# Attention inside a two-layer kernel on one core: where the maximum is subtracted, how the rows are summed, and when they are divided

## What is computed

```python
q = _split_heads(query @ Wq.T + bq)          # 16 heads, D_K = 8
k = _split_heads(key @ Wk.T + bk)
v = _split_heads(value @ Wv.T + bv)
scores = jnp.einsum('bhqd,bhkd->bhqk', q, k) / np.sqrt(D_K)
scores = jnp.where(mask[:, None, :, :] == 0, jnp.float32(-1000000000.0), scores)
p_attn = jax.nn.softmax(scores, axis=-1)
attn = jnp.einsum('bhqk,bhkd->bhqd', p_attn, v)
x = attn.transpose(0, 2, 1, 3).reshape(B, S, D_MODEL)
return x @ Wo.T + bo
```

## Time and profile before

| | |
|---|---|
| median of three runs | 1567.44 us |
| the profiled execution: its own time (span) | 1567.5 us |
| TensorE matmul busy | 1337.5 us |
| VectorE busy | 1011.9 us |
| ScalarE busy | 872.6 us |
| GpSimd busy | 716.2 us |
| mean granted TensorE clock | 0.921 |

### The profile page before, as it was taken

The page is one execution under the profiler, slowest core; times in us unless marked ns, Lnnn a source line. Parts: engine busy times, 40 slices in busy tenths (PEclk is TensorE's granted clock), DMA queues, the critical chain, the costliest instruction groups (busy, mean ns, idle before and its releaser), DMA issues.

```text
span 1567.5 us, 25069 instructions
## 1 busy us (share of the span) xinstructions
PE 1337.5 (85%) x6350; PEld 979.1 (62%) x6350; DVE 1011.9 (65%) x2377; ACT 872.6 (56%) x2421; POOL 716.2 (46%) x971
## 2 busy tenths in 40 slices
PE   7778988889978898879888899888998898896884
PEld 5556766667656766557666676666666576574552
DVE  6866675856668476766758566585666857574442
ACT  5535764556744575447655466455664477553652
POOL 3533554435534355444634355344553446442342
PEclk9979997999989899999989899799997999996765
DMA  3310000000000000000000000000000000000000
GB/s 99 108 41 4 5 9 15 4 6 7 5 14 4 7 8 6 16 6 8 4 20 2 9 4 10 14 4 8 8 6 14 5 9 5 6 3 7 4 4 4
DMA packets 34084, 20.48 MB, mean 13 GB/s; under 512 B 3624, under 2 KB 31888, under 8 KB 33936
## 3 DMA queue, kind: packets, MB, share of 16 engines
q1 hardware_dynamic: 33936, 18.81, 4.2%
HBM read 16.70 MB, written 2.10 MB: 12 GB/s over the span
## 4 chain that ended last, share of the span: by engine, by line
PE 45%; DVE 20%; issue 15%; POOL 10%; ACT 8%; DVEq 1%; POOLq 0%; SPq 0%; DMA 0%; ACTq 0%
PE M L1034 5%; PE U L1051 5%; PE U L877 4%; DVE h_lo L743 4%; PE U L881 4%; PE U L878 4%; PE Y L877 3%; ACT big L648 3%; PE Y L881 3%; PE M L1021 3%; DVE h L739 3%; PE Y L878 2%; PE M L1041 2%; PE M L1065 2%; POOL big L549 2%
## 5 line engine op out<-in xcount | busy, mean ns | idle before, releaser
L743 DVE TENSOR_TENSOR h_lo<-h,h_hi 128x512 fp32r<-128x512 f32 x384 | 316.9, 828 | 72.6 <-POOL h_hi L508 60.0
L508 POOL TENSOR_SCALAR h_hi<-h 128x512 fp32r<-128x512 f32 x256 | 180.5, 707 | 257.7 <-ACT h L609 230.0
L648 ACT ACTIVATE big<-big,nmax 128x128 f32<-128x128 f32 x512 | 199.8, 395 | 88.8 <-DVE nmax L841 88.3
L609 ACT ACTIVATE h<-U,biasT 128x512 f32<-128x512 f32 x256 | 175.9, 687 | 102.5 <-PE U L881 88.9
L549 POOL TENSOR_TENSOR big<-big,rinv 128x512 f32<-128x512 f32 x128 | 150.3, 1174 | 151.7 <-DVE rinv L844 151.7
L1051 PE MATMUL U<-big,Vr 128*128 128x512 f32 x256 | 150.9, 674 | 24.0 <-ACT big L653 24.0
L1034 PEld LDWEIGHTS M<-kT,qT 8*128 8x128 f32 x944 | 116.1, 189 | 84.3 <-issue 69.6
L1034 PE MATMUL M<-kT,qT 8*128 8x128 f32 x944 | 138.7, 286 | 2.2 <-ACT sg L666 2.1
L877 PE MATMUL U<-xn_hi,w_hi 128*128 128x512 f32 x256 | 119.3, 466 | 21.9 <-DVE h L739 12.9
L844 DVE RECIPROCAL rinv<-rsum 128x4 f32<-128x4 f32 x128 | 22.7, 177 | 174.4 <-ACT big L648 174.4
L619 ACT ACTIVATE h_hi<-h 128x512 fp32r<-128x512 f32 x128 | 80.9, 632 | 84.6 <-DVE h L739 81.7
(11 more groups left out here) (210 smaller groups left out, 3023.9 us busy)
## 6 DMA issues: line engine op xcount, KB each, us to landing
big<-in_L_xattn_W SPq DMA_DIRECT2D x16, 256.0 KB, 3.0
big<-in_L_ffn_w SPq DMA_DIRECT2D x12, 256.0 KB, 2.8
xin<-in_x SPq DMA_DIRECT2D x8, 256.0 KB, 2.7
nat<-in_ctx SPq DMA_DIRECT2D x8, 256.0 KB, 3.2
ctx<-in_ctx SPq DMA_DIRECT2D x32, 64.0 KB, 1.8
mask_sb<-in_mask_BxSxS_if SPq DMA_DIRECT2D x32, 64.0 KB, 1.9
out_dram<-xatt SPq DMA_DIRECT2D x32, 64.0 KB, 1.6
big<-in_L_ffn_w_down SPq DMA_DIRECT2D x1, 176.0 KB
```

The costliest lines, as they stand in the source:

```text
L508: nc.gpsimd.tensor_scalar(h_hi[i % 4][:, :], h32[i % 3][:, :], 1.0, 0.0, ALU.mult, ALU.add).then_inc(hi_done, 1)
L609: nc.scalar.activation(h32[i % 3][:, :], U[i % 2][:, :], ACT.Relu, bias=biasT[:, i:i + 1]).then_inc(relu_done, 1)
L648: done = nc.scalar.activation(p, p, ACT.Exp, bias=nmax[:, u % 2, r:r + 1], accum_out=rsum[:, u % 2, r:r + 1])
L743: nc.vector.tensor_tensor(h_lo[i % 4][:, :], h32[i % 3][:, :], h_hi[i % 4][:, :].bitcast(fp32), ALU.subtract).then_inc(lo_done, 1)
```

## The change

The `exp` step now runs on GpSimd and ScalarE: GpSimd adds the negative maximum to the 128x512 block in place, and ScalarE takes one exponential over the whole block without a sum. The step `rsum` is gone. The transposes wait for the exponential. The `pv` step multiplies the blocks as they are, not yet normalised, in eight matmuls instead of one: for each head h the product with its 32 columns of `Vr` into rows 32h to 32h+31 of `OA` (now 128 columns wide), and then for each head the product with a strip of `ones_r` into the same rows of `OS`, the next 128 columns of the same bank. The strip has ones in the 8 columns that belong to unit r, so that `OS` collects each head's row sum in the same places as `OA` its values. The `ot` step moves to VectorE: reciprocal of `OS`, times `OA`. The exponential stands at half step 2 after the scores in both tables, where two of four stood at 1 before.

```diff
-      "s": (4, 7, 11, 14), "exp": (1, 1, 2, 2), "rsum": 2, "pt": 5, "pv": 7, "ot": 21, "wo": 25,
+      "s": (4, 7, 11, 14), "exp": 2, "pt": 5, "pv": 7, "ot": 21, "wo": 25,
...
-      "s": (5, 8, 11, 15), "exp": (1, 1, 2, 3), "rsum": 3, "pt": 5, "pv": 7, "ot": 22, "wo": 24,
+      "s": (5, 8, 11, 15), "exp": 2, "pt": 5, "pv": 7, "ot": 22, "wo": 24,
...
-        nmax, rsum, rinv = (sb(n, [P, 2, HB]) for n in ("nmax", "rsum", "rinv"))
+        nmax = sb("nmax", [P, 2, HB])
+        ones_r = sb("ones_r", [P, 32 + 3 * DK])
...
-        OA = U[2]
+        OA, OS = U[2][:, 0:P], U[2][:, P:2 * P]
...
-                    elif what == "rsum":
-
-                        pool.wait_ge(rsum_done, g1 * H + (i + 1))
+                    elif what == "exp":
+
+                        pool.wait_ge(nmax_done, g1 * H + (i + 1))
                         p = pr[i % 2].rearrange("p (h k) -> p h k", h=HB)
-                        nc.gpsimd.tensor_tensor(p, p, rinv[:, i % 2, :].unsqueeze(2).broadcast_to([P, HB, S]), ALU.mult).then_inc(norm_done, 1)
+                        nc.gpsimd.tensor_tensor(p, p, nmax[:, i % 2, :].unsqueeze(2).broadcast_to([P, HB, S]), ALU.add).then_inc(shifted, 1)
...
-                        u, r = i // HB, i % HB
-                        if r == 0:
-                            act.wait_ge(nmax_done, g1 * H + (u + 1))
-                        p = pr[u % 2][:, r * S:(r + 1) * S]
-                        done = nc.scalar.activation(p, p, ACT.Exp, bias=nmax[:, u % 2, r:r + 1], accum_out=rsum[:, u % 2, r:r + 1])
-                        if r == HB - 1:
-                            done.then_inc(exp_done, 1)
+                        act.wait_ge(shifted, g1 * H + (i + 1))
+                        nc.scalar.activation(pr[i % 2], pr[i % 2], ACT.Exp).then_inc(exp_done, 1)
...
-                    elif what == "ot":
-
-                        act.wait_ge(oa_full, g1 * TG + (i + 1))
-                        for q in range(HB):
-                            rows = slice(32 * q, 32 * q + 32)
-                            done = nc.scalar.activation(OT[rows, :], OA[rows, q * P:(q + 1) * P], ACT.Copy)
-                        done.then_inc(oa_emptied, 1)
...
+            setup(nc.vector.memset(ones_r[:, :], 0.0))
+            nc.vector.memset(ones_r[:, 3 * DK:4 * DK], 1.0)
...
-                    elif what == "rsum":
-                        dve.wait_ge(exp_done, g1 * H + (i + 1))
-                        nc.vector.reciprocal(rinv[:, i % 2, :], rsum[:, i % 2, :]).then_inc(rsum_done, 1)
+                    elif what == "ot":
+                        dve.wait_ge(oa_full, g1 * TG + (i + 1))
+                        link1(nc.vector.reciprocal(OT[:, :], OS))
+                        nc.vector.tensor_tensor(OT[:, :], OA, OT[:, :], ALU.mult).then_inc(oa_emptied, 1)
...
-                            pe.wait_ge(norm_done, g1 * H + (i + 1))
+                            pe.wait_ge(exp_done, g1 * H + (i + 1))
...
-                        ins = nc.tensor.matmul(OA[:, :], Vr[:, r, :], pT[i % 2], start=(r == 0), stop=(r == HB - 1))
+                        for dst, w in ((OA, Vr[:, r, :]), (OS, None)):
+                            for h in range(HB):
+                                rows = slice(32 * h, 32 * h + 32)
+                                ins = nc.tensor.matmul(dst[rows, :], w[:, rows] if w is not None else ones_r[:, (3 - r) * DK:(3 - r) * DK + 32], pT[i % 2][:, h * P:(h + 1) * P],
+                                                       start=(r == 0 and w is not None), stop=(r == HB - 1), skip_group_check=True)
```

More of the change, by code:

```diff
@@ L37 @@
 Z_SETUP, M_SETUP = 1, 4
-CHAIN0, CHAINP, CHAIN1 = 3, 3, 52
+CHAIN0, CHAINP, CHAIN1 = 3, 3, 56
 CHAIN_GATES = 2
@@ L145, in attention_order @@
             put(t + first, "s", u)
-            for h, later in enumerate(where["exp"]):
-                put(t + first + later, "exp", u * HB + h)
-            for what in ("rsum", "pt", "pv"):
+            for what in ("exp", "pt", "pv"):
                 put(t + first + where[what], what, u)
@@ L309, in flamingo_kernel @@
         cap_made, oa_full, oa_emptied = sem("cap_made"), sem("oa_full"), sem("oa_emptied")
-        nmax_done, exp_done, rsum_done, norm_done = sem("nmax_done"), sem("exp_done"), sem("rsum_done"), sem("norm_done")
+        nmax_done, shifted, exp_done = sem("nmax_done"), sem("shifted"), sem("exp_done")
         pool_gates, pool_passed, dve_passed = sem("pool_gates"), sem("pool_passed"), sem("dve_passed")
```

## The result

The changed kernel takes 1629.49 us (median of four runs, 1626.71 to 1633.8) against 1567.18 us for the kernel before on the same chip: a ratio of 1.0386, with an interval of 1.0348 to 1.0423. It is **62 us slower**. The forecast was 1527 us, faster. The time lies inside the range (1485 to 1650), but only because the range reached up to a rival (strips that don't overlap, 1644 us) which, as will be seen, isn't what happened.

The account below looks back on a forecast made before the run. The prediction held the first attention stretch nearly bound by TensorE, the others by one unit's time from scores to product. From 1567.5 us: 41 less relief, 8 more division, 7 less product, giving 1527 us; range 1485 to 1650.

Parts of the forecast that it names:

- The way through the unit: Attention unit, from end of maximum to transposes: 3.15 us before, 1.9 us after, so 1.2 us less.
- The relief of 41 us: Shorter exponentials and end-of-group waits: 5 us less in each of seven walks, 6 in the last; bounds nothing to 68 us.
- The product on PE: Product with values and ones in strips on TensorE: 0.77 us a unit instead of 0.86, 7 us less altogether.
- 9.4 units of 16: Units per walk whose product on TensorE was taken to lie on the chain, from 6.5% of 124 us.
- ACT: ScalarE loses 251 us of 873 busy, to near 620; wide exponential 0.63 us; what follows in its queue comes sooner.
- DVE: VectorE's division, once for each of 32 tiles, reciprocal 0.97 us: 40 us of work, taken as 8 us more time.
- PE's waits at the end of the group: TensorE's waits for the copy behind a transpose (1.87 us) and POOL (0.97 us): shorter by about 1.2 us per unit.
- the last walk: The eighth walk, attention alone after the last experts: 6 us less from the shorter way through a unit.
- no overlap: Rival: column strips on TensorE run one after the other, 1.88 instead of 0.86 us a unit; 1644 us, chance 0.25.
- All four strips: Rival: all four strips run together on TensorE with nothing between, 0.54 us a unit; 1500 us, chance 0.20.
- DVE becomes the hold: Rival: VectorE's division holds scores and splits behind it and costs its full 40 us; 1580 us, chance 0.06.
- no relief: Rival: waits of ACT and DVE cost nothing while PE is busy, so relief is nothing; 1579 us, chance 0.07.

Follow-up runs that it names:

- shift1_exp3: Changed kernel with GpSimd's addition as its own step at half step 1 and the exponential at 3, same work: 1530.28 us, 0.9783 of the kernel before.
- strips_alone: Kernel before with only its product with the values in four column strips and one copy to OT for four: 1553.78 us, ratio 0.993.
- no_reciprocal: Changed kernel with four biased ScalarE exponentials instead of GpSimd's addition, and a cheap addition replacing the reciprocal (wrong results): 1504.82 us, 0.9607 of the kernel before.
- ones_x4: Changed kernel with the product with ones issued four times, sums four times too large: 1612.68 us, 1.0259 of the kernel before.

## Why the prediction was wrong

**The step that failed** is the pair of sentences "What follows it in the queue, above all the ReLU of the experts, comes sooner" and "POOL has the same count and kind of work in the same place of its queue, so nothing but its wait changes". Count and kind were the same, 128 operations on 128x512. But who waits for them was turned round. Before, GpSimd's product stood behind the exponential and only TensorE's transposes, three half steps later in the loop, needed it. Now ScalarE needs it at once, at the same half step. The way through the unit was added up from durations alone (1.04 + 0.63 + 0.25 = 1.9 us), as if GpSimd were free when the maximum is done. In the stretch shown, the maximum ended at 750.02 and the exponential at 755.97: 5.95 us. That was a bad case, but the mean is no better: from the end of the maximum to the block that TensorE transposes it took 4.60 us before (end of GpSimd's product) and takes 4.60 us now (end of the exponential), where 1.2 us less were forecast. And the ReLU came 0.86 us behind its product on average where it came 0.42 us before: not sooner but later. The relief of 41 us became a loss. With the same terms and a place that lets GpSimd come first (shift1_exp3) the kernel takes 1530 us, which is near the forecast of 1527; that they meet is partly luck, since several terms were off.

The other terms:

- *The product on PE*, 0.77 us taken between 0.55 and 0.99: it is 0.57, all four strips together, the lower bound. The starts stand 6 to 7 ns apart. The Trainium skill (TensorE: Matmul & The Clock Gate, Part 3) gives a packed group the time of one matmul and about 4 ns for each further tile, and the trace agrees but for the 6 to 7 ns. Its other sentence there, that a weight load overlaps only with a matmul in other row groups, the trace doesn't bear out: the loads for the second four records start at 746.87 to 746.89 us, while matmuls of the same strips, each 297 ns long from 746.84 us on, are under way. I gave the seen pair of row strips too much weight. What it is worth in time isn't shown for this kernel: strips_alone saves 0.50 us a unit on PE, 64 us in all, and is 11 to 14 us faster (with three copies to `OT` saved beside it), so a saving on PE counted for about a fifth there, where the prediction counted 9.4 units of 16.
- *ACT*: busy 720.2 us where I wrote near 620. The exponential is 630 ns, as predicted, but the groups that I subtracted overlap each other: the old exponentials and their reads cover 221.1 us of ScalarE together, not 199.8 + 98.8. With that the sum is 698 us; the last 22 us aren't accounted for. Summing groups overstated what ScalarE would gain; no term of the time used it.
- *DVE*: reciprocal 953 ns against 0.97 predicted; VectorE's wait for it 20.5 us. Of the 8 us that I took for the division, no_reciprocal, which saves 0.67 of its 1.25 us, shows about 5. VectorE's wait for ScalarE's exponentials is gone, as said.
- *PE's waits at the end of the group* were to shrink. The one for the copy behind the transposes did, from 24.0 to 13.4 us over the whole run, but the one for the projection's copy grew by 28.6 us. In the last walk, for which I took 6 us, 3.4 came: 139.9 us from the end of the last expert product where it was 143.3.
- *The rivals*: "no overlap" gave 1644 us, near the result, by a mechanism that didn't occur. "All four strips" was right on the price and wrong on the time. "DVE becomes the hold" was wrong by no_reciprocal, and "no relief" didn't reach the time either. The rival that was missing is "ScalarE waits at the head of its queue for GpSimd". Its parts were in sight: both steps carry the name `exp` and thus one place, and GpSimd already waited 230 us for ReLUs.

What remains open: how the 62 us divide between waits and lower clock beyond the 17 us of ones_x4, why strips_alone gave 11 to 14 us and not more, and whether filler works through the clock alone.

## What to carry to other kernels

Before adding up the way through a chain of engines, look at what stands in front of each link in its own queue, and at what stands behind the consumer; an operation that is cheap on an idle engine is dear when another engine waits for it at the head of its queue. Where every engine walks through one common order, try a producer on another engine at least one place ahead of its consumer: here one half step was worth 69 to 84 us, and two 99, with the same instructions. When a change comes out slower, take it apart before dropping it: sums by ones, strips and division together were worth 3.6% once the detour over GpSimd was gone.

## What the runs showed of the hardware that I had not expected

- Four fp32 column strips of 32 output rows, each with its own weights and data, start 6 to 7 ns apart, and eight records take 0.24 us. Sixteen, with the change of layout, take 0.57 us where one product of 512 columns took 0.86. Weight loads of the second four records ran under the matmuls of the first four.
- More work on TensorE made a kernel faster: 3072 further records (141.1 us busy for 54.8) brought 1.0386 down to 1.0259, while the granted clock went from 0.888 to 0.947. Like filler cost 20 and 29 us in kernels where TensorE is idle less (218 and 261 us, against 286). That the clock is the reason isn't shown.
- An exponential on 128x128 with bias takes 397 ns, and the wide one on 128x512 takes 630. Narrow ones overlap: in the whole run four of them in place of one make ScalarE busy 76 us more (791.6 for 715.4), 0.6 us a unit, and cost only about 12 us of time.
